# Leaving out an engine's wait for its own previous instruction at sixteen kinds of instruction, in a fused attention and quantized FFN kernel

## The reference

```python
def _L0_attn_ref(x, w_qkv, w_out):
    qkv = (x @ w_qkv).reshape(b, s, 3, H, DH)            # H 16, DH 64
    scores = jnp.einsum('bihd,bjhd->bhij', q, k) * scale
    allowed = (j <= i) & (j > i - WINDOW)                # WINDOW 128
    scores = jnp.where(allowed, scores, -jnp.inf)
    attn = jax.nn.softmax(scores, axis=-1)
    out = jnp.einsum('bhij,bjhd->bihd', attn, v).reshape(b, s, d)
    return out @ w_out

def bitlinear(x, W, b):
    w_scale = jnp.clip(jnp.mean(jnp.abs(W)), EPS, None)
    Wq = jnp.clip(jnp.round(W / w_scale), -1.0, 1.0) * w_scale
    x_scale = jnp.clip(jnp.max(jnp.abs(x), axis=-1, keepdims=True), EPS, None)
    xq = jnp.clip(jnp.round(x * (QB / x_scale)), -QB - 1.0, QB) * (x_scale / QB)
    return jnp.einsum('bnd,hd->bnh', xq, Wq) + b

x = x + _L0_attn_ref(_layernorm(x), w_qkv, w_out)
x = x + bitlinear(gelu(bitlinear(_layernorm(x), W1, b1)), W2, b2)
```

## Time and profile before

| What | Value |
|---|---|
| median of 3 runs | 3287.9 us |
| the profiled execution's own time | 3286.34 us |
| its span, first to last instruction of the slowest core | 3284.8 us |
| spans of the 8 cores | 3269.0 to 3284.8 us |
| granted TensorE clock, cores 0 to 7 | 0.847 to 0.851 |
| TensorE matmul busy | 2268.7 us, 69% |
| VectorE busy | 2086.2 us, 64% |
| ScalarE busy | 1138.9 us, 35% |
| chain that ended last | PE 54%, DVE 21%, ACT 12%, issue 7%, DMA 4% |

### The profile page before, as it was taken

The page is one execution under the profiler, slowest core; times in us unless marked ns, Lnnn a source line. Parts: engine busy times, 40 slices in busy tenths (PEclk is TensorE's granted clock), DMA queues, the critical chain, the costliest instruction groups (busy, mean ns, idle before and its releaser), DMA issues.

```text
span 3284.8 us, 43104 instructions; the slowest of 8 cores (3269.0 to 3284.8 us)
## 1 busy us (share of the span) xinstructions
PE 2268.7 (69%) x13196; PEld 1067.3 (32%) x13196; DVE 2086.2 (64%) x3711; ACT 1138.9 (35%) x2064; POOL 17.8 (1%) x36
## 2 busy tenths in 40 slices
PE   0366666666666565666656388888888888888886
PEld 0133333333333333333333133333333333333332
DVE  1345545545545656566565577787878778777775
ACT  1344545545534444443443222222222222222221
POOL 0000000000000000000000000000000000000000
PEclk9886787787777686776867599999999999999999
DMA  4221122122111111122222400000000000000000
GB/s 163 83 68 65 58 71 65 58 71 65 65 46 55 59 58 51 54 68 81 71 71 68 146 31 26 26 26 19 20 26 26 26 26 26 26 26 26 17 23 20
DMA packets 94361, 170.83 MB, mean 52 GB/s; under 512 B 41138, under 2 KB 41394, under 8 KB 93619
## 3 DMA queue, kind: packets, MB, share of 16 engines
q1 hardware_dynamic: 84480, 125.86, 12.3%
q10 hardware_dynamic: 5044, 25.44, 2.2%
q0 software_dynamic: 4608, 16.78, 1.3%
HBM read 126.09 MB, written 41.95 MB: 51 GB/s over the span
## 4 chain that ended last, share of the span: by engine, by line
PE 54%; DVE 21%; ACT 12%; issue 7%; DMA 4%; DVEq 1%; ACTq 1%; SPq 0%; POOLq 0%
PE psC L1184 15%; PE psA L979 8%; PE psB L979 7%; PE psA L550 5%; ACT hqT L1168 4%; PE psB L550 4%; PE psC L783 4%; DVE probs L711 3%; PE psC L550 3%; DVE cells L655 2%; DVE cells L660 2%; DVE wqch L426 2%; ACT qT L603 2%; ACT probsT L743 2%; DVE sgnA L417 1%
## 5 line engine op out<-in xcount | busy, mean ns | idle before, releaser
L1184 PE MATMUL psC<-W2qT,hqT 128*128 128x512 bf16 x2048 | 485.6, 389 | 127.1 <-ACT hqT L1168 127.1
L1184 PEld LDWEIGHTS psC<-W2qT,hqT 128*128 128x128 bf16 x2048 | 191.7, 99 | 372.1 <-issue 175.3
L979 PE MATMUL psA<-W1qT,xqT 128*128 128x512 bf16 x1024 | 256.1, 395 | 0.0
L1003 DVE TENSOR_REDUCE cells<-h_sb 128x1 f32<-128x1024 f32 x128 | 156.2, 1220 | 148.7 <-ACT h_sb L996 138.7
L979 PE MATMUL psB<-W1qT,xqT 128*128 128x512 bf16 x1024 | 243.2, 380 | 0.0
L760 PE MATMUL psC<-probsT,v_hist 128*64 128x128 bf16 x1024 | 75.7, 291 | 223.9 <-ACT probsT L743 223.9
L951 DVE TENSOR_TENSOR tib<-t1a,tfb 128x1024 f32<-128x1024 f32 x160 | 196.1, 1225 | 16.6
L711 DVE TENSOR_SCALAR probs<-probs,cells 128x256 bf16<-128x256 bf16 x512 | 146.6, 286 | 56.2 <-DVE probs L711 1.0
L568 DVE CAST k_sb<-psB 128x1024 bf16<-128x1024 f32 x32 | 39.2, 1224 | 221.6 <-PE psB L550 221.6
L1168 ACT ACTIVATE hqT<-psD 128x1024 bf16<-128x1024 bf16 x64 | 65.6, 1024 | 320.0 <-PE psD L1158 320.0
L1168 ACT ACTIVATE hqT<-psF 128x1024 bf16<-128x1024 bf16 x64 | 65.6, 1024 | 319.1 <-PE psF L1158 319.1
(11 more groups left out here) (159 smaller groups left out, 3723.6 us busy)
## 6 DMA issues: line engine op xcount, KB each, us to landing
wstage<-w SPq DMA_DIRECT2D x256, 256.0 KB, 2.6
xin<-xc SPq DMA_DIRECT2D x32, 512.0 KB, 4.0
x1sp<-x1b SPq DMA_DIRECT2D x32, 512.0 KB, 3.0
y<-outbuf POOLq DMA_DIRECT2D x32, 512.0 KB, 4.7
x1b<-x1sp SPq DMA_DIRECT2D x22, 512.0 KB, 4.0
w2td<-w2st SPq DMA_DIRECT2D x64, 128.0 KB, 2.0
W2qT<-w2td ACTq DMA_DIRECT2D x4, 2048.0 KB, 13.9
wstgA<-wqkv ACTq DMA_DIRECT2D x8, 768.0 KB, 4.3
```

The source lines that it names most:

```text
L979: e.matmul(out=p[:, nn * 512:(nn + 1) * 512], lhsT=xqT[:, cc * 128:(cc + 1) * 128], rhs=W1qT[:, cc * HF + jj * 1024 + nn * 512: cc * HF + ...
L1003: op("dve", lambda e, jj=j, c=cl: e.tensor_reduce(out=c[:, FH + jj:FH + jj + 1], in_=h_sb[:, jj * 1024:(jj + 1) * 1024], axis=AX.X, op=ALU ...
L1184: pv = op("pe", lambda e, nn=n, kk=k: e.matmul(out=psC[:, nn * 512:(nn + 1) * 512], lhsT=hqT[:, kk * 128:(kk + 1) * 128], rhs=W2qT[:, kk * ...
```

## The change

`op` takes a new argument `nosync`, and the writer leaves out the wait for the engine's own predecessor where it is set. It is set at sixteen kinds of instruction: on ScalarE the copies `xlnT`, `q_sb`, `qT` and `kT_hist`, `probsT`, `i1row`, `xqT`, `i2row` and `hqT`, the exponentials of heads 1 to 3 of a group, and gelu; on VectorE the copies `k_sb`, `v_hist` and `attnout`, the second row maximum of a group (L660), the scaling of heads 1 and 3 of a group (L711), and the row maximum of `h_sb` (L1003). Where an instruction of the list waits for another engine, that wait stays.

Two more things change. The scaling of heads 0 and 2 now waits by name for the reciprocal in front of it, and keeps the wait for its predecessor, which is the same reciprocal. And the scores of groups 2 and 3, which waited half by half for the exponentials that free their PSUM (head 1 for the first half, head 3 for the second), now wait for head 3 ahead of the first half.

```diff
-        def op(ek, fn, waits=(), inc=None, amt=1, is_dma=False):
+        def op(ek, fn, waits=(), inc=None, amt=1, is_dma=False,
+               nosync=False):
...
             v = op("act", lambda e, p=sp: e.copy(out=xlnT, in_=p),
-                   waits=[(sP, pv), (sP, ms.get(("qkv", t - 1, 2), 0))], inc=sA)
+                   waits=[(sP, pv), (sP, ms.get(("qkv", t - 1, 2), 0))],
+                   inc=sA, nosync=True)
...
         def a_scores(t, g):
...
-            pev = ms[("expv", t, g - 2)] if g >= 2 else None
             w0 = [(sA, ms[("qT", t)]), (sA, ms[("kT", t)]),
-                  (dC, ms["consts_ld"])]
-            if pev is None:
-                w0.append(psum_free[pfk])
+                  psum_free[pfk], (dC, ms["consts_ld"])]
             pv = None
+            first = True
             for half in range(2):
-                first = True
-                wh = list(w0) if half == 0 else []
-                if pev is not None:
-                    wh.append((sA, pev[half * 2 + 1]))
+                wh = w0
...
         def a_sm_max(t, g):
...
-                waits=[(sP, ms[("scores", t, g)])], inc=sV)
+                waits=[(sP, ms[("scores", t, g)])], inc=sV, nosync=True)
         def a_sm_exp(t, g):
...
-                    inc=sA)
+                    inc=sA, nosync=(hh > 0))
         def a_sm_norm(t, g):
...
-            op("dve", lambda e, c=cl, g_=g: e.reciprocal(
+            r0 = op("dve", lambda e, c=cl, g_=g: e.reciprocal(
...
-                waits=[(sA, ev[1])])
+                waits=[(sA, ev[1])], inc=sV)
+            rc = r0
...
-                    op("dve", lambda e, c=cl, g_=g: e.reciprocal(
+                    rc = op("dve", lambda e, c=cl, g_=g: e.reciprocal(
...
-                    inc=sV)
+                    waits=[(sV, rc)], inc=sV, nosync=(hh in (1, 3)))
...
 def _emit_all(nc, OPS, _ES, cut=None):
...
-                if zs is not None and zi > 0:
+                if zs is not None and zi > 0 and not ns:
                     eng.wait_ge(zs.h, zi)
```

More of the change, by code:

```diff
@@ L576, in a_qkv @@
                     waits=[(sP, pv), (sP, ms.get(("av", t - 1, 3), 0))],
-                    inc=sV)
+                    inc=sV, nosync=True)
                 ms[("v_sb", t)] = v
@@ L709, in a_sm_norm @@
                                CEL_SUMS + 4 * g_ + 4]),
-                        waits=[(sA, ev[3])])
+                        waits=[(sA, ev[3])], inc=sV)
                 v2 = op("dve", lambda e, c=cl, g_=g, hh_=hh: e.tensor_scalar(
@@ L743, in a_pt @@
             v = op("act", lambda e, g_=g, p=sp: e.activation(
-                out=probsT[g_ % 2], in_=p, func=AF.Copy), waits=wv, inc=sA)
+                out=probsT[g_ % 2], in_=p, func=AF.Copy), waits=wv, inc=sA,
+                nosync=True)
             psum_free[key] = (sA, v)
@@ L774, in a_outproj @@
                    waits=[(sP, ms[("av", t, 3)]),
-                          (sP, ms.get(("outproj", t - 1), 0))], inc=sV)
+                          (sP, ms.get(("outproj", t - 1), 0))], inc=sV,
+                   nosync=True)
             ms[("attnout", t)] = v
@@ L1006, in emit_gelu @@
                 op=ALU.max, apply_absolute_value=True),
-                waits=[(sA, va)])
+                waits=[(sA, va)], nosync=True)
         def f_front_dve(t):
@@ L1064, in f_front_pe @@
                 out=invs1row, in_=psF[0:1, 0:128], func=AF.Copy),
-                waits=[(sP, pv)], inc=sA)
+                waits=[(sP, pv)], inc=sA, nosync=True)
             ms[("i1r", t)] = va
@@ L1080, in f_front_pe @@
                 out=xqT, in_=p, func=AF.Copy),
-                waits=[(sP, pv), (sP, ms.get(("w1", t - 1, 3), 0))], inc=sA)
+                waits=[(sP, pv), (sP, ms.get(("w1", t - 1, 3), 0))], inc=sA,
+                nosync=True)
             psum_free[key] = (sA, v)
@@ L1242, in _emit_all @@
         tot = {}
-        for (k, waits, fn, inc, amt, is_dma) in OPS:
+        for (k, waits, fn, inc, amt, is_dma, ns) in OPS:
             if inc is not None:
@@ L1246, in _emit_all @@
         OPS = [(k, [(s, min(v, tot.get(s.name, 0))) for (s, v) in waits],
-                fn, inc, amt, is_dma) for (k, waits, fn, inc, amt, is_dma) in OPS]
+                fn, inc, amt, is_dma, ns)
+               for (k, waits, fn, inc, amt, is_dma, ns) in OPS]
     def mk(ek):
```

13 lines of the change are left out of this document (7 added, 6 removed).

## The result

The changed kernel takes 3208.4 us (median of 10 runs) against 3291.2 (10 runs of the kernel before beside them): ratio 0.9758, 95% interval 0.9726 to 0.979. By that ratio 80 us are gone (69 to 90) where 59 were forecast; 3208 lies inside the range of 3204 to 3277, and 3 us past the fast end of the forecast's own range (3211). The gain was forecast and its place too; the forecast size was a quarter short of the measured one.

A forecast was written before the change was run, and what follows sets the result against it. Bound: in attention a chain of waits through VectorE, then alternating TensorE and ScalarE; in FFN, TensorE with five hand-overs. 49 + 10 = 59 us off 3286.3 gave 3227.6, median 3229; range 3204 to 3277, own range 3211 to 3259.

The forecast's parts named there:

- The chain of a tile and the 31 hand-overs from tile to tile: Attention: VectorE's stretch, then alternating TensorE and ScalarE up to `v_hist`; a tile's gain counts 31 times, 49 us together.
- Kind (a): Wait between two instructions of one engine: leaving it out gives 0.15 us, ends 0 and 0.20 on VectorE.
- VectorE's part: Attention tile from `v_hist` to group 2's scaling: ten waits left out, 1.50 us, less 0.45 for doubled ones, net 1.05.
- Kind (b): Satisfied wait behind a pending one: 0.075 us on VectorE, 0.06 on ScalarE; six doubled waits lose 0.45 a tile.
- Kind (c): Satisfied wait ahead of a pending one, as at the reciprocal on VectorE: costs nothing.
- what was cover: Attention work off the chain: faster exponentials, `k_sb` and `attnout` and the scores' moved wait, all costed at nothing.
- The alternating part: Attention, TensorE and ScalarE in turn, up to `v_hist`: 0.30 + 0.12 + 0.075 us saved a tile.
- FFN: Five hand-overs TensorE to ScalarE per tile lose a needless wait: 0.30 us, times 32 = 10 us; ends 0 and 24.
- TensorE's clock: Rival, attention's q product: tighter tiles move where the clock rises, 51 us either way, 3280 or 3178; chance 0.08.
- VectorE starts no earlier: Rival: VectorE's instructions keep their start-to-start distance without the wait, doubled waits still cost; 3276 us; chance 0.17.
- The chain moves: Rival: within VectorE's part the chain switches to ScalarE's exponentials or TensorE's transposes, half of 33 us lost: 3245; chance 0.10.
- slower through the scores: Rival: group 2's first half comes too late for VectorE, up to 41 us idle, 3317; scores' wait and slower 0.05.

The follow-up runs named there:

- run with more waits left out: Changed kernel without the scaling's doubled waits, predecessor's wait left out at further attention instructions of VectorE and head 0's exponential on ScalarE: 3083.4 us, ratio 0.938.
- FFN run: Kernel before, with the change's left-out waits in the FFN stage alone: ratio 0.9967 (0.9938 to 0.9995), 11 us.

## Why the prediction was right, and where its size was off

- **The chain of a tile and the 31 hand-overs from tile to tile**: right. The 31 intervals gave 58.6 us where 49 were forecast, and 100 in the run with more waits left out, where prices times count along this chain were 110. The last tile has no next one and was left out of the count; it gave 2 us more.
- **Kind (a), 0.15 us between neighbours**: mis-sized. It is 0.19 on VectorE by the medians and 0.18 to 0.20 in ScalarE's rows. With 0.195 VectorE's part is 10 x 0.195 - 0.45 = 1.5 a tile, 46.5 us (44 with the medians and 0.08 for the doubled wait); measured 47.4, forecast 33. This is the largest error. I had ScalarE's row with the right number and split the difference with an end that nothing in the trace asked for.
- **Kind (b)**: right, and I put a loss where one was. 0.075 forecast, 0.08 to 0.09 measured for each doubled wait on VectorE; on ScalarE's hand-overs 0.06 forecast, 0.054 measured.
- **Kind (c) and what was cover** (exponentials, scores, `k_sb`, `attnout`): right; the scores by an experiment of their own.
- **The alternating part**: 0.495 x 31 = 15 forecast, 11.9 + 7.4 = 19 measured. At 0.195 for its two neighbours 18 are expected.
- **FFN**: mis-sized, 10 forecast, 15 measured in the trace of the change and 14 in that of the FFN run (11, with 2 to 20, by its time). The 160 hand-overs gave 8.7 and the waits for the two rows, missing from my sum, 2.5; the rest fits the clock.
- **TensorE's clock**: I gave it as a rival of either sign with 51 us at most. It came as a loss of 8 us inside a larger gain. It is no case of its own but a term of every change of this stage, from 6 to 19 us in four runs. It also helped the range: without these 8 us the time would have come out near 3200, below the range's end of 3204, so the errors of the other terms were partly hidden by one that I had put at nothing in the sum.
- **VectorE starts no earlier** was given 0.17 and is false here. The Trainium skill's page "VectorE: DVE Perf Modes" says in its section "The DRAIN you can't avoid" that a semaphore after each of eight chained copies cost nothing over one after the last. These traces don't agree with it as a rule for waits: two neighbours without a wait between them start 0.19 us closer, and the time follows. The same section says that a next operation which isn't held back starts earlier, and with that they agree.
- **The chain moves** and **slower through the scores** did not happen.

Worked out again with the measured prices: 46.5 + 18 + 1 - 8 + 2 for the last tile + 15 in FFN = 74 to 75. The median spans of the cores compared above differ by 75.5 (3277.8 and 3202.3 us), and the measured 80 has an interval of 10 either way. Core 5 alone differs by 66, since its stretch ahead of the first `v_hist` took 6 us more after the change (the medians 1.5 more) and its FFN stage gave 12 us and not 15. Why cores differ so in these two places is not shown.

## What to carry to other kernels

In this kernel a wait for the engine's own predecessor cost 0.19 us for each short instruction (0.15 to 0.7 us) on the chain, and a second wait for the same value another 0.08. So keep that wait only where the next instruction depends on the last one, reading what it wrote for instance, and write it once. If the trace has even one neighbour pair without the wait, on any engine, take its number rather than a cautious mean. And price a change of spacing by the matmul group behind it as well: where TensorE mostly waits, its clock level at the next large product can cost as much as the waits that were saved, and a few matmuls without use ahead of it can be worth more than either.

## What the hardware showed that I had not expected

Adding 0.5 us of wait per tile on VectorE cost 36 us in 31 tiles: 15 are the waits themselves, and nearly 19 came because TensorE's clock rose later, with more of the q and k products' matmuls recorded at 631 ns and not at 379. And six matmuls without use in each tile, most of them at the lower level, recorded there at 0.63 us each and 0.43 apart, made a kernel 56 us faster while lifting the granted clock of the attention stage from 0.75 to 0.83.
